# A layer with experts: rows turned by DMA transposes, one expert number at a time, and a reordered last stage

## What is computed

```python
xn = _layernorm(x, axis=-1)                      # x: 8 x 512 x 256
x = x + attn(xn, W_kqv, b_kqv, W_proj, b_proj, slopes) + ffn(xn, Wg, W1, W2)

def ffn(x, Wg, W1, W2):                          # T = 4096 tokens, 8 experts
    probs = softmax(xt @ Wg)
    _, top_idx = top_k(probs.T, cap)             # each expert picks cap = 512 tokens
    tok2exp = ...                                # one expert for each token
    for e in range(E):
        gate = where(tok2exp == e, weights, 0.0)
        h = gelu(xt @ W1[e]) @ W2[e]             # 256 -> 512 -> 256
        out = out + gate[:, None] * h
```

## Time and profile before

| | us |
|---|---|
| three executions | 737.09, 731.8, 734.67 |
| median | 734.67 |
| the profiled execution: its time | 732.48 |
| the profiled execution: its span, first to last instruction | 730.4 |
| TensorE busy in the span | 583.8 (80%) |
| VectorE, ScalarE, GpSimd busy | 431.1, 332.7, 331.2 |

### The profile page before, as it was taken

The page is one execution under the profiler, slowest core; times in us unless marked ns, Lnnn a source line. Parts: engine busy times, 40 slices in busy tenths (PEclk is TensorE's granted clock), DMA queues, the critical chain, the costliest instruction groups (busy, mean ns, idle before and its releaser), DMA issues.

```text
span 730.4 us, 13964 instructions
## 1 busy us (share of the span) xinstructions
PE 583.8 (80%) x4711; PEld 350.6 (48%) x4712; DVE 431.1 (59%) x861; ACT 332.7 (46%) x625; POOL 331.2 (45%) x483
## 2 busy tenths in 40 slices
PE   1977696668889899898667989886886789898892
PEld 1544353334345345354234455351445677787782
DVE  4663538968996887968969757741222234343341
ACT  3553652047564656556435556655631223332230
POOL 5555111224443543434324558867434555554531
PEclk9999899879999999999899999998998899999997
DMA  4799685842322512424113426325931233332210
GB/s 130 213 226 191 227 279 199 275 139 65 91 77 80 154 59 93 119 71 142 52 52 90 148 85 211 97 79 187 369 117 61 84 95 87 103 97 79 85 38 1
DMA packets 79687, 92.14 MB, mean 126 GB/s; under 512 B 10562, under 2 KB 68867, under 8 KB 79623
## 3 DMA queue, kind: packets, MB, share of 16 engines
q1 hardware_dynamic: 69264, 69.82, 32.0%
q0 software_dynamic: 6672, 17.91, 7.5%
q10 hardware_dynamic: 3696, 3.67, 1.9%
HBM read 49.60 MB, written 40.18 MB: 123 GB/s over the span
## 4 chain that ended last, share of the span: by engine, by line
PE 47%; DVE 25%; issue 9%; ACT 7%; DMA 3%; POOL 3%; another core or an unknown queue 3%; SPq 1%; POOLq 0%; DVEq 0%; ACTq 0%
DVE mx L824 10%; PE ps L1239 9%; PE ps L1140 7%; PE ps L1251 7%; PE ps L1044 6%; PE ps L1126 5%; PE ps L1115 4%; PE ps L1096 4%; ACT pr_all L708 3%; DVE mx L819 3%; PE ps L1093 2%; ACT pr_all L636 2%; DVE rec_wide L843 1%; PE ps L1224 1%
## 5 line engine op out<-in xcount | busy, mean ns | idle before, releaser
L708 ACT ACTIVATE pr_all<-ps 128x512 f32<-128x512 f32 x320 | 181.2, 599 | 186.0 <-PE ps L1115 169.1
L824 DVE TENSOR_REDUCE mx<-ps 128x2 f32<-128x768 f32 (+1 forms) x192 | 157.1, 861 | 50.2 <-PE ps L1096 47.9
L578 POOL TENSOR_SCALAR_AFFINE_SELECT pr_all<-pr_all 128x384 f32<-128x384 f32 x128 | 64.6, 530 | 184.8 <-ACT pr_all L708 184.7
L1115 PE MATMUL ps<-qs,ks 128*128 128x512 f16 (+2 forms) x448 | 117.9, 336 | 20.7 <-ACT pr_all L708 13.5
L1096 PE MATMUL ps<-ks,qs 128*128 128x384 f16 (+3 forms) x512 | 117.8, 316 | 0.0
L1093 PE MATMUL ps<-maxmask,idb 128*128 128x256 bf16 (+1 forms) x320 | 84.7, 265 | 34.7 <-DVE mx L824 19.9
L1126 PE MATMUL ps<-pr_all,vt 128*17 128x512 f32 (+3 forms) x1024 | 88.9, 467 | 2.7 <-POOL pr_all L581 2.7
L1239 PE MATMUL ps<-pr_all,xnp 128*128 128x128 f16 x960 | 83.3, 227 | 8.9 <-DVE pr_all L997 8.5
L1140 PE MATMUL ps<-wp,yn 128*128 128x256 f32 x256 | 70.3, 402 | 13.7 <-DVE xr L849 8.0
L1239 PEld LDWEIGHTS ps<-pr_all,xnp 128*128 x960 | 68.3, 99 | 25.3 <-issue 12.6
L718 ACT ACTIVATE pr_all<-ps 128x512 f32<-128x512 f32 x40 | 23.9, 598 | 121.8 <-PE ps L1239 91.6
(11 more groups left out here) (178 smaller groups left out, 859.2 us busy)
## 6 DMA issues: line engine op xcount, KB each, us to landing
qs<-q_parts SPq DMA_DIRECT2D x64, 100.0 KB
ks<-k_parts SPq DMA_DIRECT2D x64, 96.0 KB
sorted_rows<-ecmp POOLq DMA_DIRECT2D x1, 5160.0 KB, 21.1
pr_all<-sorted_rows SPq DMA_DIRECT2D x40, 129.0 KB
k_parts<-pr_all SPq DMA_DIRECT2D x16, 256.0 KB, 2.9
q_parts<-pr_all SPq DMA_DIRECT2D x16, 256.0 KB, 2.9
xr<-in_L_attn_x_dram SPq DMA_DIRECT2D x8, 512.0 KB
w_h<-in_L_ffn_W_dram SPq DMA_DIRECT2D x16, 256.0 KB
```

The source lines that it names most:

```text
L578: pool.affine_select(out=v, in_=v, compare_op=ALU.is_ge, fill=0.0, base=0, pattern=[[0, 3], [1, P]], channel_multiplier=-1).then_inc(sel_m ...
L708: act.activation(dst, src, ACT.Exp, scale=SCORE).then_inc(exp_made, 1)
L824: last = dve.tensor_reduce(mx[:, n1 % 2, :, 2 * g + c, t], ps[:, 2 * (u % 2):2 * (u % 2) + 2, c0:c0 + w], AX, ALU.max)
L1115: last = pe.matmul(out, ks[:, p, c, t * P:(t + 1) * P], rhs, start=True, stop=True, skip_group_check=True)
```

## The change

- `xs_sb` and the turning on PE and DVE are gone. SP issues one DMA transpose for each tile (`load_rows`), which writes `xT` in its turned form; `xT` has eight slots instead of two. PE's up(s) waits for that DMA. Banks 0 and 1 are free in this stage.
- The token numbers and gates come by a DMA of their own, 8 bytes for each of 128 rows (`load_tokens`). At the start SP issues eight transposes and eight of these ahead of `store_sum`; later the transpose of tile s + 3 stands ahead of the tokens of tile s.
- Four banks take the second product's output in turn (`OUT_BANKS`), so down(s) waits for combine(s - 4) and not for combine(s - 2).
- DVE's order is low(s + 1), then combine(s).
- PE loads a group's word at the group's start, and the next group's word behind up of the sixth tile of the group; each expert's number is worked out shortly before its use.
- The last four of the 16 matmuls of the last batch row's product stand behind up(1).
- POOL clears the gather buffer before it waits for the stored sum, and gathers four tiles ahead instead of six.
- 39 tiles are worked through (`WORK`), not 40.

```diff
 CAP = T // X
 SLOTS = 8
-AHEAD = 6
+AHEAD = 4
+OUT_BANKS = (4, 5, 0, 1)
+
+ROWS_FIRST = 3
 TILES = NT + X
+
+WORK = TILES - 1
 HG = 4
 NG = H // HG
...
+        xT = cut(8 * 4 * P * 2, F16, "p (q a c) -> p q a c", q=8, a=4)
+        token = cut(8 * 2 * 4, I32, "p (q c) -> p q c", q=8)
         hg = cut(2 * FF * 4, F32, "p (q c) -> p q c", q=2)
         hh = cut(2 * 2 * FF * 2, F16, "p (q a c) -> p q a c", q=2, a=2)
...
-            def load_tile(s, k, q):
-                sp.dma_start(xs_sb[:, q, :].bitcast(I32), xs_d[bass.ds(s * P, P), :]).then_inc(xs_in[q], 16)
+            def load_rows(s, q):
+                sp.dma_start_transpose(out=xT[:, q], in_=xs_d[bass.ds(s * P, P), 0:2 * E]).then_inc(xT_in[q], 16)
+
+            def load_tokens(s, q):
+                sp.dma_start(token[:, q, :], xs_words[bass.ds(s * P, P), E:E + 2]).then_inc(xs_in[q], 16)
 
             sp.wait_ge(y_made, NG * B - 1)
             for q in range(SLOTS):
-                load_tile(q, 0, q)
+                load_rows(q, q)
+                if q % 2:
+                    load_tokens(q - 1, q - 1)
+                    load_tokens(q, q)
             store_sum(B - 1)
-            with sp.Fori(1, TILES // SLOTS) as k:
+            for s in range(SLOTS, SLOTS + ROWS_FIRST):
+                sp.wait_ge(h_made, s - SLOTS + 1)
+                load_rows(s, s % SLOTS)
+            with sp.Fori(1, WORK // SLOTS) as k:
                 for q in range(SLOTS):
+                    s = k * SLOTS + q
+                    sp.wait_ge(h_made, s + ROWS_FIRST - SLOTS + 1)
+                    load_rows(s + ROWS_FIRST, (q + ROWS_FIRST) % SLOTS)
                     sp.wait_ge(ob_out[q], k * 16)
-                    load_tile(k * SLOTS + q, k, q)
+                    load_tokens(s, q)
+            for s in range(WORK // SLOTS * SLOTS, WORK):
+                if s + ROWS_FIRST < WORK:
+                    sp.wait_ge(h_made, s + ROWS_FIRST - SLOTS + 1)
+                    load_rows(s + ROWS_FIRST, (s + ROWS_FIRST) % SLOTS)
+                sp.wait_ge(ob_out[s % SLOTS], 16 * (WORK // SLOTS))
+                load_tokens(s, s % SLOTS)
             for q in range(SLOTS):
-                sp.wait_ge(ob_out[q], 16 * (TILES // SLOTS))
+                sp.wait_ge(ob_out[q], 16 * (WORK // SLOTS + (q < WORK % SLOTS)))
 
 
...
+            mark(pool.memset(xg[:, :, :], 0.0))
             pool.wait_ge(xa_out, 16 * B)
-            mark(pool.memset(xg[:, :, :], 0.0))
             for q in range(AHEAD):
                 tile_c(q, 0, q)
-            with pool.Fori(0, TILES // SLOTS - 1) as k:
+            with pool.Fori(0, WORK // SLOTS) as k:
                 for q in range(SLOTS):
                     s2 = q + AHEAD
                     tile_c(k * SLOTS + s2, k + s2 // SLOTS, s2 % SLOTS)
                     scatter_c(k * SLOTS + q, k, q)
-            k = TILES // SLOTS - 1
-            for q in range(SLOTS):
+            k = WORK // SLOTS
+            for q in range(WORK % SLOTS):
                 s2 = q + AHEAD
-                if s2 < SLOTS:
+                if s2 < WORK % SLOTS:
                     tile_c(k * SLOTS + s2, k, s2)
                 scatter_c(k * SLOTS + q, k, q)
...
                 for q in range(2):
                     gelu(2 * k + q, q)
+            gelu(WORK - 1, (WORK - 1) % 2)
 
 
...
-                dve.scalar_tensor_tensor(out=ob[:, q, :], in0=bank[4 + q % 2][:, 0:E],
-                                         scalar=xs_sb[:, q, 2 * E + 2:].bitcast(F32), in1=xg[:, q, :],
+                dve.scalar_tensor_tensor(out=ob[:, q, :], in0=bank[OUT_BANKS[q % len(OUT_BANKS)]][:, 0:E],
+                                         scalar=token[:, q, 1:2].bitcast(F32), in1=xg[:, q, :],
                                          op0=ALU.mult, op1=ALU.add).then_inc(ob_made, 1)
 
-            def steps(s, k, tiles, more=SLOTS):
+            def steps(s, k, tiles=SLOTS):
                 for q in range(tiles):
+                    if q + 1 < tiles or tiles == SLOTS:
+                        low(s + q + 1, (q + 1) % 2)
                     combine(s + q, k, q)
-                    if q < more + 1:
-                        low(s + q + 1, (q + 1) % 2)
-                    if q < more - 1 or more == SLOTS:
-                        take_x(s + q + 3, (q + 1) % 2)
 
             invert(NG * B - 2)
-            take_x(0, 0)
-            take_x(1, 1)
             invert(NG * B - 1)
+            low(0, 0)
...
-                steps(k * SLOTS, k, SLOTS)
-            steps(TILES - SLOTS, TILES // SLOTS - 1, SLOTS, SLOTS - 2)
+            steps(0, 0)
+            with dve.Fori(1, WORK // SLOTS) as k:
+                steps(k * SLOTS, k)
+            steps(WORK // SLOTS * SLOTS, WORK // SLOTS, WORK % SLOTS)
 
 
...
 
-            def turn_x(s, k, q):
-                pe.wait_ge(xs_in[q], k * 16 + 16)
-                for j in range(4):
-                    last = pe.transpose(bank[q % 2].bitcast(F16)[:, j * P:(j + 1) * P], xs_sb[:, q, j * P:(j + 1) * P], id16[:, :])
-                last.then_inc(tt_made, 1)
-
-            def experts_of(k, count=SLOTS):
-                code = pe.value_load(codes[0:1, bass.ds(k, 1)], min_val=0, max_val=X ** SLOTS - 1)
-                return [pe.snap((code // X ** j) % X, min_val=0, max_val=X - 1) for j in range(count)]
-
-            def up(s, q, e):
-                pe.wait_ge(xT_made, s + 1)
+            def experts_of(k):
+                return pe.value_load(codes[0:1, bass.ds(k, 1)], min_val=0, max_val=X ** SLOTS - 1)
+
+            def expert(code, j):
+                return pe.snap((code // X ** j) % X, min_val=0, max_val=X - 1)
+
+            def up(s, k8, q8, e):
+                q = q8 % 2
+                pe.wait_ge(xT_in[q8], k8 * 16 + 16)
                 after(pe, hg_made, s - 1)
                 terms = [(0, 0), (0, 1), (1, 0)]
...
-                after(pe, ob_made, s - 1)
+                after(pe, ob_made, s - len(OUT_BANKS) + 1)
                 w2p = (w2_h, w2_l)
                 for f in range(FC):
                     for j, (a_, b_) in enumerate([(0, 0), (0, 1), (1, 0)]):
-                        last = pe.matmul(bank[4 + q][:, 0:E], hh[:, q, a_, f * P:(f + 1) * P],
+                        last = pe.matmul(out[:, 0:E], hh[:, q, a_, f * P:(f + 1) * P],
                                          w2p[b_][:, bass.ds(e, 1), f * E:(f + 1) * E].rearrange("p x w -> p (x w)"),
                                          start=(f == 0 and j == 0), stop=(f == FC - 1 and j == 2))
...
             pe.wait_ge(w1_in, 32)
-            first = experts_of(0, 2)
-            up(0, 0, first[0])
-            turn_x(2, 0, 2)
+            code = experts_of(0)
+            first = [expert(code, j) for j in range(2)]
+            up(0, 0, 0, first[0])
             pe.wait_ge(xadd_made, TB * (B - 1))
-            for groups in ((0, 1, 2), (3,)):
+            def last_row(groups):
                 for t in range(TB):
                     project(B - 1, t, groups, bank[7 - 2 * (t // 2)][:, t % 2 * E:(t % 2 + 1) * E], begin=(t % 2 == 0))
-            up(1, 1, first[1])
+
+            last_row((0, 1, 2))
+            up(1, 0, 1, first[1])
+            last_row((3,))
             pe.wait_ge(w2_in, 32)
             pe.wait_ge(y_copied, NG * B)
 
-            def steps(s, k, more=SLOTS):
-                experts = experts_of(k) + (experts_of(k + 1, 2) if more == SLOTS else [])
-                for q in range(SLOTS):
-                    down(s + q, q % 2, experts[q])
-                    if q < more:
-                        up(s + q + 2, q % 2, experts[q + 2])
-                    if q < more - 1 or more == SLOTS:
-                        turn_x(s + q + 3, k + (q + 3) // SLOTS, (q + 3) % SLOTS)
+            def steps(s, k, tiles=SLOTS):
+
+                code = experts_of(k)
+                e = [expert(code, j) for j in range(2)]
+                for q in range(tiles):
+                    down(s + q, q, e[q])
+                    if q == 0:
+                        e.append(expert(code, 2))
+                    if q + 2 < tiles or tiles == SLOTS:
+                        up(s + q + 2, k + (q + 2) // SLOTS, (q + 2) % SLOTS, e[q + 2])
+                        if q == SLOTS - 3 and tiles == SLOTS:
+                            code = experts_of(k + 1)
+                        if q + 3 < tiles or (tiles == SLOTS and q + 3 < SLOTS + 2):
+                            e.append(expert(code, (q + 3) % SLOTS))
 
             steps(0, 0)
-            with pe.Fori(1, TILES // SLOTS - 1) as k:
+            with pe.Fori(1, WORK // SLOTS) as k:
                 steps(k * SLOTS, k)
-            steps(TILES - SLOTS, TILES // SLOTS - 1, SLOTS - 2)
+            steps(WORK // SLOTS * SLOTS, WORK // SLOTS, WORK % SLOTS)
```

36 lines of the change are left out of this document (13 added, 23 removed).

## The result

The changed kernel took 739.91 us in the median (735.2 to 742.54, 20 executions), the kernel before, on the same chip, 735.71 (20 executions): a ratio of 1.0055, 95% interval 1.0036 to 1.0074. I had forecast 716.5, with a range of 703 to 735. It is half a per cent slower where 2.5% faster was forecast.

The account below looks back on a forecast made before the run. PE was taken to bound the last stage, at 3.36 us a tile. Gains of 4.1 + 3.4 + 7.5 + 1.2 + 2.0 = 18.2 us from 732.5 gave 714.3, plus 2.2 to the median: 716.5 us, range 703 to 735.

Parts of the forecast that it names:

- The three stops go too: Fourth rival: the last stage's unnamed stops, 13.4 us, vanish with the loads or DVE chain, giving 705 us; chance 0.10.
- the stops themselves I leave as they are: Last stage: three unnamed stops of 6.2, 3.3 and 3.9 us were assumed to stay unchanged.
- POOL issues a gather and a scatter per tile: Last stage: POOL's two issues at 1.32 us each take 2.64 of 3.14 us per tile, so POOL would not bound.
- The turning: Last stage: taking four matmuls, 0.22 us a tile, off PE's chain for about 34 tiles gains 7.5 us.
- third rival: Up is limited by address arithmetic and split loads cost as much as joined ones: 727 us at most, 723 likelier; chance 0.12.
- The expert numbers: Group heads: splitting the loads of expert numbers gains 0.4 us for each of three heads, 1.2 us.
- four banks and the copy: After stops in the last stage: up no longer waits for DVE's copy, 2.0 us; banks give nothing in quiet periods.
- The start: Start of the last stage: low(1) ahead of combine(0) puts PE one tile further at 562.5, gaining 4.1 us.
- the fortieth tile: End of PE's chain: leaving out the empty last tile saves a whole period, 3.4 us.
- The transposes: SP and DMA queues: a transpose may take 1.8 us of SP and 1.8 us of all queues, and stays hidden.
- first rival: DMA transposes become the bound, deciding from 4.54 us a tile; at 5.2 us the time is 760.6 us; chance 0.08.
- second rival: SP's transpose issue, at 3 us each, holds back the last sum's store by 9.7 us: 726 us; chance 0.12.

Follow-up runs that it names:

- g5: Changed kernel with reordered first DVE group, expert numbers inside down, unrolled PE loop, early group codes and no expert-stage indirect DMAs: 687.73 us, ratio 0.9310 to the kernel before.
- e2: Changed kernel with the turning back on TensorE, plain loads for transposes and copies on VectorE: 704.94 us, ratio 0.9911 to the kernel before.
- f2: Changed kernel with all expert numbers of a group worked out at its head again, from two loads: 702.27 us, ratio 0.9874 to the kernel before.
- c_before: The kernel before, unchanged, traced on a chip of the 712 us kind: 712.59 us, ratio 0.999 to the kernel before.
- c_after: The changed kernel, unchanged, on a chip of the 712 us kind: 703.26 us, ratio 0.9864 to the kernel before.
- e3: Changed kernel with gathers six tiles ahead instead of four: 701.93 us, ratio 0.9862 to the kernel before.
- e4: Changed kernel with VectorE's old order, combine(s) and then low(s + 1): 707.55 us, ratio 0.9938 to the kernel before.

## Why the prediction was wrong

**"The three stops go too ... I see no mechanism", and "the stops themselves I leave as they are."** This step decided the sign. The stops were the symptom of a mechanism of this kind of chip: counts of TensorE that are held while POOL's indirect DMAs run (53 us of late up counts in the changed kernel, 22 in the kernel before, none in g5 without these DMAs). I had the rows: three pieces of 13.4 us without a name, POOL's DMAs 1.3 us apart. To leave the stops as they are I would have had to ask what POOL does during them, and I did not. With the change the 34 tiles went from 132.7 to 146.4 us, where on the other kind of chip they went from 125.6 to 123.8. I put a chance on their going and none on their growing.

**"POOL issues a gather and a scatter per tile ..., 2.64 of 3.14 us. Neither becomes the bound."** The share was right and the conclusion was not. POOL did not run out of time; what it issued held up another engine's signals.

**The turning, 7.5 us.** Measured 3.3 us (e2, 2.0 of them in the 34 tiles) on the 712 us kind, and nothing at all in a quiet tile (3.40 and 3.39 us, where 3.1 to 3.2 was forecast). The step that failed is "the work is taken out of the bound engine, so I need only ask what is late next": I asked that of gelu and low, and not of TensorE's own sequencer. That was my third rival, "up is limited by its address arithmetic", at 0.12, with 723 to 727 us; as a ratio to the median of 734.7 that is 0.984 to 0.990, and on the 712 us kind 0.986 came out. The row that could have told me was the up of 1.81 us for 24 matmuls beside the down of 1.36 for 12 matmuls of twice the width: both are 3072 columns, and should take the same.

**The expert numbers, 1.2 us, and four banks and the copy, 2.0.** f2 puts the first at 0.7 us, within its error of nothing. The 34 tiles gained 1.8 us with everything, which e2 gives to the turning alone, so the second is 1 us or less; without stops there was nothing for it to gain.

**The start, 4.1 us, and the fortieth tile, 3.4.** The sizes are right: 4.2 and, with the tail, 4.1 us (c_before and c_after), on the first chip 6.5 and 4.1. The pieces of the start are not. I had the store of the last sum 1.2 us later than before; on the first chip it was issued at 550.6, 2.2 us earlier, since up(0) began before 540 and up(1) took 1.34 us for my 2.0. So the first gather began at 555.6 and down(2) at 559.9, for my 558.2 and 562.5. On the 712 us kind less of this came through: the store's landing took 4.1 us (c_after) where it had taken 2.9 (c_before). That the 4.2 agrees is in part luck. Down(2) was PE's first long wait, as said.

The transposes took 1.25 us of SP each, for the 1.8 that I had allowed, and were hidden. Their pieces were 512 of 256 bytes, as I took them, but at about 20 ns each and not 55 (16.4% of 16 x 181 us over 25136 packets of all sizes is 19 ns), so 0.6 us of all queues a tile for my 1.8. No tile came near the 4.54 us of the first rival; the second rival's store went at 550.6, on time.

On the chips where counts come in time the forecast ratio of 0.975 stands against 0.986: right in sign, with the turning's term 4 to 7 us too large.

What stays open: which edit makes the changed kernel suffer more from held counts than the kernel before. Its runs of four indirect DMAs (two sums close together, gathers four ahead, and POOL no longer waiting for rows) were the candidate, but e3 and e4, which change them, met no such chip. The traces speak for caution: in the steady part the changed kernel issues by twos where counts come in time (c_after) and mostly by fours where they don't, and the kernel before by fours in c_before and by one to three on the first chip. So the runs may be as much an effect of the late counts, which let two tiles go at once, as a cause. Whether the issue of the descriptors or their traffic holds the counts, and whether half as many would do, wasn't tried there either. What sets the two kinds of chip apart is unknown.
